# Values one step behind, and the experts' first tile inside attention

## The reference

```python
xn = layernorm(x)                                   # over the features
Q, K, V = xn @ wq + bq, ctx @ wk + bk, ctx @ wv + bv    # 16 heads of 8 features
scores = Q K^T / sqrt(8) + attn_mask + window_mask      # 128 x 128 for each batch and head
x = x + tanh(g_xattn) * (softmax(scores) @ V @ wo + bo)

xn = layernorm(x)
probs = softmax(xn @ gate_w)                        # 8 experts, the best 2 of each token
for i in range(8):                                  # weights wi, 0 where not chosen
    out += (silu(xn @ w1[i]) * (xn @ w3[i])) @ w2[i] * wi     # 128 -> 512 -> 128
x = x + tanh(g_ffn) * out
```

## Time and profile before

| | |
|---|---|
| median of 3 runs | 459.09 us (458.98 to 460.26) |
| profiled execution, its own time | 459.81 us |
| its span, first to last instruction | 458.1 us |
| TensorE busy | 407.4 us, 89% |
| VectorE, GpSimd, ScalarE busy | 290.9, 259.4, 239.6 us |
| granted TensorE clock, mean | 0.972 |

### The profile page before, as it was taken

One profiled execution on the slowest core, in us unless ns is written; L12 is line 12 of the kernel. 1 busy time (PEld: TensorE's weight loads), 2 busy tenths in 40 slices (PEclk: granted clock), 3 DMA queues, 4 the chain that ended last, 5 costly groups with the idle time before them and its releaser, 6 DMA issues.

```text
span 458.1 us, 14422 instructions
## 1 busy us (share of the span) xinstructions
PE 407.4 (89%) x4547; PEld 360.1 (79%) x4548; DVE 290.9 (64%) x786; ACT 239.6 (52%) x564; POOL 259.4 (57%) x312
## 2 busy tenths in 40 slices
PE   2879979999999998997879899988999999999970
PEld 1647658877777776776669799888999999999960
DVE  3876798887888887889546368544444554554420
ACT  2758506667677675766666534233444444444430
POOL 5743554334654737473646568776666665655560
PEclk9989979999999999999999999999999999999995
DMA  7964557457766666485223233334444343333235
GB/s 215 279 123 94 96 96 185 90 105 113 170 147 136 152 134 161 106 216 169 65 69 75 45 52 48 54 67 61 69 70 58 44 54 46 46 47 40 24 29 189
DMA packets 74783, 46.24 MB, mean 101 GB/s; under 512 B 8608, under 2 KB 71490, under 8 KB 74562
## 3 DMA queue, kind: packets, MB, share of 16 engines
q1 hardware_dynamic: 59072, 34.84, 33.2%
q0 software_dynamic: 12272, 8.92, 14.9%
q10 hardware_dynamic: 3392, 1.88, 1.7%
HBM read 18.12 MB, written 14.20 MB: 71 GB/s over the span
## 4 chain that ended last, share of the span: by engine, by line
PE 62%; DMA 9%; issue 7%; DVE 6%; ACT 6%; POOL 4%; ACTq 2%; POOLq 1%; DVEq 0%
PE ps_scores L1612 20%; PE ps_max_scores L1620 10%; DMA sums_scratch<-yt,xg 8%; PE ps_values L897 7%; PE ps_max_scores L853 6%; PE ps_scores L883 5%; PE ps_scores L837 3%; PE ps_max_scores L837 2%; POOL expert_rows_scratch L1328 2%; PE ps_out L921 1%; ACT xn L474 1%; DVE rsplit L1119 1%; ACT w_all L464 1%; DVE qkf L558 1%; POOL sums_scratch L1733 1%
## 5 line engine op out<-in xcount | busy, mean ns | idle before, releaser
L1733 POOL DMA_INDIRECT sums_scratch<-yt,xg x71 | 115.9, 1633 | 66.9 <-DMA sums_scratch<-yt,xg 28.1
L1612 PE MATMUL ps_scores<-xgT,qs 128*128 128x128 f32 x1136 | 141.1, 278 | 5.1 <-ACT xgT L1658 3.8
L1612 PEld LDWEIGHTS ps_scores<-xgT,qs 128*128 128x128 f32 x1136 | 134.1, 194 | 7.1 <-ACT xgT L1658 4.5
L1699 DVE TENSOR_TENSOR qs<-qs,ps_scores 128x512 f32<-128x512 f32 x71 | 48.8, 688 | 88.4 <-PE ps_scores L1612 70.5
L1119 DVE TENSOR_REDUCE rsplit<-ps_max_scores 128x4 f32<-128x512 f32 x128 | 84.8, 685 | 15.0 <-PE ps_max_scores L837 11.2
L1328 POOL DMA_INDIRECT expert_rows_scratch<-xr,pos x64 | 66.4, 1037 | 25.6 <-issue 13.1
L1620 PE MATMUL ps_max_scores<-w_all,qs 128*128 x568 | 75.6, 276 | 2.8 <-ACT yt L1669 2.3
L1620 PEld LDWEIGHTS ps_max_scores<-w_all,qs 128*128 128x128 f32 x568 | 69.0, 192 | 3.8 <-issue 3.6
L1027 ACT ACTIVATE pT<-ps_scores 128x1024 f32<-128x1024 f32 x64 | 62.0, 1022 | 18.1 <-PE ps_scores L837 17.8
L1662 ACT ACTIVATE qs<-ps_scores 128x512 f32<-128x512 f32 x71 | 42.3, 596 | 30.3 <-PE ps_scores L1612 30.3
L1669 ACT ACTIVATE yt<-ps_max_scores,xg 128x128 f32<-128x128 f32 x71 | 26.1, 368 | 60.4 <-PE ps_max_scores L1620 40.4
(11 more groups left out here) (202 smaller groups left out, 527.8 us busy)
## 6 DMA issues: line engine op xcount, KB each, us to landing
qs<-w_all SPq DMA_DIRECT2D x96, 64.0 KB
ks<-w_all SPq DMA_DIRECT2D x96, 64.0 KB
w_all<-in_L_ffn_w_dram SPq DMA_DIRECT2D x24, 256.0 KB
xg<-expert_rows_scratch SPq DMA_DIRECT2D x71, 65.0 KB, 1.9
xs<-in_x_dram SPq DMA_DIRECT2D x4, 512.0 KB, 5.6
sums_scratch<-xs SPq DMA_DIRECT2D x8, 256.0 KB, 4.5
sums_scratch<-yt,xg POOLq DMA_INDIRECT x71, 3.3
expert_rows_scratch<-fill SPq DMA_DIRECT2D x16, 65.0 KB, 2.5
```

The costliest lines, as they stand in the source:

```text
L1612: ins = nc.tensor.matmul(bank[u % 2][:, c * P:(c + 1) * P], w13[:, u % 2, n, c * P:(c + 1) * P], xgT[:], start=True, stop=True)
L1699: nc.vector.tensor_tensor(hidT[:, u % 2], act_s[:, u % 2], ps_b[u % 2], ALU.mult).then_inc(hid_ready, 1)
L1733: pool.indirect_dma_start(out=z_d, out_offset=bass.IndirectOffsetOnAxis(ap=xg_u[:, u, X_IDX:X_IDX + 1], axis=0), in_=yt[:, u % YRING], in_ ...
```

## The change

- The values of batch b are multiplied in the step of batch b+1, in one run of 32 matmuls. The transposes and the projection that follow move one step further back.
- The first expert tile is turned and multiplied with w1 at the end of step 30, and with w3 at the end of step 31, into the two banks of raw scores, which have no more use by then. VectorE copies its weights, normalises its rows and copies the transpose in steps 29 to 31.
- w1 and w3 of each expert are loaded from GpSimd's queue at j = 0 and 1, w2 stays in SyncE's.
- Rows are scattered as they are, out of `xs`, with their mean and the inverse of the deviation beside them (132 instead of 130 numbers). VectorE normalises each expert tile (`norm_rows`, L1736). ScalarE's `norm_rows` and `copy_choice` go.
- The second four scatters of a group take the second gate from the same place, so GpSimd first waits until the first four have landed (`second_gates`); the wait at j = 3 goes.
- The ring `yt` has 6 buffers instead of 4. The last group's scatters skip one tile.

```diff
-    YRING = 4
+    YRING = 6
...
 attend_sync: w1 and w3 no longer here, one load_w2(g - 2) after both halves of group g
...
-            def values(at, half):
+            def values(at):
...
             def step(at):
-                last, ahead = at.plus(-1), at.plus(AHEAD)
-                if at.exists():
-                    score(at)
...
+                last, out, ahead = at.plus(-1), at.plus(-2), at.plus(AHEAD)
+                if at.is_past(1):
+                    values(last)
+                if at.is_past(2):
+                    turn_attn(out)
+                if ahead.exists():
+                    score_max(ahead, range(0, 1))
+                score(at, range(0, 2))
+                if at.is_past(2):
...
+                        project(out)
+                if ahead.exists():
+                    score_max(ahead, range(1, 2))
+                score(at, range(2, 4))
+                if at.is_past(1):
+                    turn_values(last)
                 if ahead.exists():
-                    score_max(ahead, range(0, 2))
+                    score_max(ahead, range(2, 3))
                 if at.plus(2).exists():
                     turn_max(at.plus(2))
...
+                if at.known and at.b == B - 2:
+                    first_tile(0)
+                elif at.known and at.b == B - 1:
+                    first_tile(1)
...
 ScalarE
+                if at.is_past(1):
+                    copy_values(at.plus(-1))
+                if at.is_past(2):
+                    copy_attn(at.plus(-2))
+                if at.is_past(3):
+                    square(at.plus(-3))
...
+                exps(at, 0)
+                exps(at, 1)
...
 VectorE
-                for part, banks in enumerate((range(0, 1), range(1, 3), range(3, NB))):
+                for part, banks in enumerate((range(0, 1), range(1, 2), range(2, NB))):
                     if ahead.exists():
                         take_max(ahead, banks)
-                    if part == 2:
-                        split_max(ahead if ahead.exists() else None, out)
+                    if part == 0 and at.is_past(2):
+                        residual(out)
...
+                    if part == 1 and at.is_past(1):
+                        normalise(last)
...
+                if at.known and at.b >= B - 3:
+                    first_tiles(at.b - (B - 3))
...
 GpSimd
+            def second_gates(r):
+
+                pool.wait_ge(scattered[r.u], r.half * (2 * GB * 16) + GB * 16)
+                stand_alone(pool)
+                pool.tensor_copy(xs_all[:, bass.ds(r.g * GB, GB), X_GATE], gate2[:, r.u]).then_inc(second_ready, 1)
...
+            def load_weights(e, n):
+
+                for p in range(2):
+                    pool.wait_ge(qk_loaded[e % 2][p], (e // 2 + 1) * (16 * LOADS))
+                pool.dma_start(w_sb_all[:, e, n * F:(n + 1) * F], (w1, w3)[n][e]).then_inc(w_loaded[n], 16)
...
-                    scatter(sent, (range(0, 2), range(2, 5), range(5, 7), range(7, 8))[at.j])
-                if at.j == 3 and sent.exists() and (not at.known or sent.g + 2 < NG):
-                    pool.wait_ge(scattered[sent.u], sent.half * (2 * GB * 16) + 2 * GB * 16)
-                    stand_alone(pool)
+                    scatter(sent, (range(0, 2), range(2, 4), range(4, 6), range(6, 8))[at.j])
+
+                if at.j < 2:
+                    load_weights(at.g, at.j)
...
 experts
+            def first_tile(half):
+
+                if half == 0:
+                    pe.wait_ge(npT_ready, B)
+                    pe.wait_ge(res_done, B - 3)
+                    pe.wait_ge(max_taken, B * NB)
+                    turn_rows(0, 0, 0)
+                up(0, 0, range(half, half + 1))
...
+            def norm_rows(t, u, turn):
+
+                dve.wait_ge(xg_loaded[u], turn * 16 + 16)
+                if not (isinstance(t, int) and t < 2):
+                    dve.wait_ge(xg_turned, t - 1)
+                nc.vector.tensor_scalar(xh[:, u % 2], xg[:, u, 0:D], xg[:, u, X_MEAN:X_MEAN + 1],
+                                        xg[:, u, X_STD:X_STD + 1], ALU.add, ALU.mult).then_inc(xh_ready, 1)
```

More of the change, by code:

```diff
@@ L751, in batches, with each_batch @@
                 step(At(B // UNROLL - 1, c))
+        def each_batch(step):
+            for b in range(B):
+                step(At(b // UNROLL, b % UNROLL))
         class Group:
@@ L910, in turn_attn @@
                 pe.wait_ge(attn_ready, at.b + 1)
+                if not at.plus(3).exists() and (r := route(at.plus(1), 3)):
+                    pe.wait_ge(rank_taken, r.g + 1)
                 if at.is_past(1):
@@ L1230, in step @@
                             nc.vector.tensor_copy(cnt[:], ps_l[:, 0:E]).then_inc(count_taken, 1)
+                    if part == 1 and at.is_past(1):
+                        normalise(last)
+                    if part == 2:
+                        if ahead.exists():
+                            split_max(ahead)
+                        if (r := route(at, 2)):
+                            scale_gap(r)
                     if chosen:
@@ L1693, in experts_scalar, with experts_vector @@
             copy_out(act, 1)
[L1695 removed]
+        def experts_vector(dve):
             def gated(t, u, turn):
```

431 lines of the change are left out of this document (208 added, 223 removed).

## The result

The changed kernel takes 466.03 us (median of 4 runs, 464.37 to 469.84), the kernel before 459.08: ratio 1.016, 95% interval [1.009, 1.022]. It is slower; the forecast was 455.2. The profiled execution of the changed kernel took 464.37, its span is 462.7 in place of 458.1.

What follows compares the result with a forecast made beforehand. TensorE was taken to bound attention, GpSimd's sends the early tiles. Steps -2.0, joint -3.0 and early tiles +1.1 gave -3.9 from 459.81, so 455.9, as a median 455.2 us; range 446 to 465, the forecast's own 450 to 458.

Steps and rivals of the forecast that it cites:

- The joint: End of attention to the start of tile 2: less TensorE idle and shorter steps, -3.0 us, bounds -5 and 0.
- In the changed order the first half of tile 0 fills the shadow: Joint: tile 0's halves run during the exponentials of steps 30 and 31, so 3.4 us of idle go.
- The 0.6 for turn, copy and multiply: End of step 30: 0.6 us new in which TensorE has nothing else to do.
- The steps: Attention: a step goes from 4.97 to 4.90 us net, -2.0 us for 28 steps, bounds -13 and +6.
- a plain loop of 4.70: Attention step: values and scores wait for both exponentials on ScalarE, a round of 4.65 to 4.75 us, taken as 4.70.
- What the merged values save: Attention step on TensorE: one run of values saves an estimated 0.3 us, beside 0.2 for a gap behind a transpose.
- The early tiles: Tiles 2 to 24: -5.6 for the ring, +4.5 and +0.2 for sends, +2.0 for GpSimd's remaining work; sum +1.1 us.
- sends 5 and 6: Early tiles: with six buffers these also wait for all before, 4.1 us each instead of 1.86, together +4.5 us.
- The last long wait for the ring: Early tiles: six buffers move the last wait from tile 22 to tile 24 or 25, worth -5.6 us.
- the change adds nothing to TensorE in the last stretch: Tiles 25 to 69: left at their time of 125.75 us, 2.79 each.
- GpSimd: Rival: dearer loads and later landings make GpSimd the bound in attention, 463.2 us or 466, chance 0.25.
- the prediction's estimate from it: Rival for tiles 1 to 18: VectorE's new operation locks GpSimd, +2.5 us, 458; chance 0.17 together with no difference.

Runs made afterwards that it cites:

- after: The changed kernel, unedited, in its first profiled execution: 464.37 us, median of its runs 466.03, ratio to the kernel before 1.016.
- after_again: The changed kernel, unedited, timed again beside the kernel before: 471.0 us, ratio 1.023.
- last_early_5: The changed kernel with the last expert's w1 and w3 issued by GpSimd in steps 26 and 27, not 28 and 29: 463.4 us, ratio to the kernel before 1.007.
- fifth group: Runs on one chip: kernel before 460.4 us, changed kernel unedited 466.4, changed kernel with the last expert's w1 and w3 issued in steps 26 and 27 463.4.
- second pair: Two further traces, the changed kernel unedited (471.0 us) and the kernel before unedited (458.4 us), run in the same group.
- before: The kernel before the change, unedited: median 459.08 us, profiled execution 459.81.
- before_again: The kernel before, unedited, run again for a trace from the same chip as three other kernels: 458.4 us.
- pool_loads: The kernel before with only w1 and w3 issued by GpSimd at j = 0 and 1 of each group, w2 by SyncE: 461.4 us, ratio 1.002.
- fourth group: Runs on one chip with slower transfers: kernel before 486.4 us, changed kernel unedited 500.6, and three edits of the changed kernel 499.4, 495.2 and 500.7.
- loads_sync: The changed kernel with all w1 and w3 issued by SyncE beside w2, none by GpSimd: 502.1 us, ratio to the kernel before 1.034.
- after_4: The changed kernel, unedited, as control: 466.4 us, ratio to the kernel before 1.011; its trace is of its slowest run, 479.59.

## Why the prediction was wrong

**The joint (forecast -3.0, measured +3.7).** This is the step that failed: 6.7 of the 8.5 us between the forecast of -3.9 and the measured +4.6 in span. "In the changed order the first half of tile 0 fills the shadow" fits the traces of after, after_again and last_early_5, in which no wait for exponentials stands in the joint, but tile 0's place was not timed where transfers are fast. The 0.6 for turn, copy and multiply came out at 1.2 of idle in last_early_5 (0.42 and 0.80). What the sum left out is a wait that the change adds: VectorE's first copy now stands in step 29 and asks for weights that GpSimd issues in steps 28 and 29. The prediction moved the loads, priced their issue and asked who waits for SyncE; it did not ask when the last of them lands against the first reader, which the same change moves two steps forward. With the loads two steps earlier the joint is 1.2 to 1.4 us shorter than before (31.93 and 31.62 against 33.1 and 33.02). So -3.0 was too much even then: idle fell from 7.3 to 5.2, not to 4, with 1.5 us of waits for VectorE's maxima that the joint of before didn't have, and the work counted in the joint did not fall. In time the early loads gave less than in the joint (about 2 us in the fifth group, with overlapping intervals), so the 5 us are shown for the joint only.

**The steps (forecast -2.0, measured +1.45 and +6.5).** First a mistake of counting: 107.35 to 206.79 are VectorE's marks of steps 7 and 26, so 19 steps of 5.23, not 20 of 4.97. In the prediction's own measure steps went from 4.97 to 4.90 (97.96 us from 109.09 to 207.05 over 20), exactly the forecast; in true steps, from 5.23 to 5.16. That is luck: in the second pair the same measure went up, from 4.88 to 4.98. With 19 steps VectorE is also busy 4.26 us a step, not 4.05, and a group of before lasts 20.9 us, not 19.9. The loss that repeats lies ahead of that stretch: from the mark of step 0 to that of step 7 the old order took 33.99, 33.99 and 34.27 us (before, before_again, pool_loads), the new one 36.92 and 38.60 (after, after_again), 36.64 and 37.26 with the early loads. In the first trace 2.2 of it are three waits for the maxima's transfer. That wait stands nowhere in the prediction. The forecast compared a plain loop of 4.70 with a mean that holds all delays; the plain steps were 4.73 before and are 4.80 now, so the loop through the exponentials was right in kind (4.70 by forecast) and there was nothing to gain from it. What the merged values save is 0.06 of TensorE a step (1.65 in 26), not 0.3.

**The early tiles (forecast +1.1, measured +0.6 from tile 2 to the end, +2.1 in the second pair).** Its parts came nearly as written: sends 5 and 6 stand 4.4 and 4.2 behind the one before, send 0 is at 5.2 behind tile 2 as before, and the lost time up to tile 28 fell by 2.4. The last long wait for the ring is at tile 25, as named. Wrong was "the change adds nothing to TensorE in the last stretch": from tile 28 to the end 3.05 are lost. Tile 33 waits for rows that are asked for 7.9 us later; from the transpose of tile 32 to that of tile 33 are 3.59 us in place of 2.79, so this wait is 0.8 of the loss, and the rest, spread over other tiles, isn't explained.

**GpSimd (rival, 463.2 to 466, chance 0.25).** Its sum is off by one: -2 + 6, -3.0 + 1.5 and +1.1 + 1.5 give +5.1, not +4.1, so 464.2 to 467. The time fell into it, for another reason. GpSimd is not the bound: its load issue is 0.59 us, not 1.0 or 1.9, no wait of TensorE in steps 0 to 26 ends with GpSimd, and GpSimd's own idle time is 3.1 us in all before the eight copies of the second gates. The move alone changed nothing (1.002 [0.999, 1.005]). Its harm is where it puts the last load. What 14 loads do to the small transfers is no price of the move, since the kernel before makes the same loads from SyncE.

**Issuing engines and the port pair.** What the Trainium skill says of issuing engines (DMA: Bandwidth & Descriptors, Issuing engines are not separate DMA queues), that only issue time is saved, fits pool_loads: the loads moved to GpSimd, the time the same (1.002). By what the Trainium skill says of the shared port pair (SBUF — State Buffer, Who interferes with whom), a `tensor_scalar` can hold it for the whole instruction and block GpSimd; the prediction's estimate from it was 2.5 us more on the sends. No run shows that cost here. VectorE's new operation takes 0.34 us 71 times, and a send 1.555 us as the median, 1.556 before; all 71 sends take 115.7 us, 115.9 before.

**What stays open.** Whether the early loads are worth 2 us or the 5 of the joint: the intervals overlap. Why the maxima's transfer lands late in steps 4 to 7, and how much of the rest of the loss in steps 0 to 7 it causes. What stretches the transfers in three of the five groups, and why the changed kernel loses 3% there and 1 to 2% otherwise. In the fourth group its wait for `qs<-npT` is 10.9 us (12.0 with the early loads), which is not all of the 14, and no trace of the kernel before was taken in such a group to compare with.

## What to carry to other kernels

When a load and its first reader both move, price the landing against the reader: a wait for "all weights" in an in-order queue holds up everything behind it, and TensorE's clock may fall with it. Compare like with like: a loop without delays against the plain steps, not against the mean, and count the marks. A small transfer in a busy stretch can be critical although no row of before shows a wait for it; the time from its issue to its use (here 6.5 us in a plain step) is a number to read. And a gain in one stretch of a trace is not yet a gain in time: take both.

## What the runs showed of the hardware

Four of the 12 KB transfers that ScalarE issues among bulk loads let TensorE go on only 7.3 to 8.4 us after their issue in the first trace of the changed kernel. A plain load of 256 KB costs GpSimd 0.59 us to issue as the median of 16, where SyncE needs 0.39 (before) to 0.42 (loads_sync). After 2.98 us in which TensorE stood still, eight matmuls took 2.08 us in place of 1.06 and 32 small ones 1.94 in place of 1.08; the full rate was back some 6 us after the first matmul. In after_4, after 2.66 us, the same eight still took 1.16, and the 32 behind them 1.70.
